# A two-layer transformer kernel: the start of the second attention rearranged (own share by a matrix product, first low part by GpSimd, last normalization one batch later)

## What is computed

```python
xn = _layernorm(x, axis=-1)
s = _L0_attn_ref(xn, ...)              # 16 heads, attention within each token
g = _silu(_L0_ffn_ref(xn, ...))        # 15 experts + last expert's share combine * xn + shared part
x = x + s * g
xn = _layernorm(x, axis=-1)
s = _L1_attn_ref(xn, gamma, w_qkv, w_out)   # rms norm, 16 heads of 64, softmax over 1024 keys
g = _silu(_L1_ffn_ref(xn, ...))
x = x + s * g
```

## Time and profile before

| what | value |
|---|---|
| median of three runs | 1123.43 us (1122.56 to 1123.49) |
| the profiled execution | 1122.48 us, of which its span is 1120.4 us |
| TensorE busy | 1100.0 us, 98% of the span |
| VectorE, GpSimd, ScalarE busy | 847.6, 794.2, 590.7 us |
| granted TensorE clock | 1.000 of full speed |
| stretch of the change | about 311 to 375 us |

### The profile page before, as it was taken

How to read it: one execution, slowest core, us unless ns; L and a number is a source line. 1 busy time by engine, 2 the same in 40 slices (tenths; PEclk the granted TensorE clock), 3 DMA queues, 4 the chain that set the end, 5 groups by cost and what they waited for, 6 DMA issues and landing times.

```text
span 1120.4 us, 21168 instructions
## 1 busy us (share of the span) xinstructions
PE 1100.0 (98%) x8397; PEld 705.2 (63%) x8397; DVE 847.6 (76%) x1250; ACT 590.7 (53%) x936; POOL 794.2 (71%) x522
## 2 busy tenths in 40 slices
PE   9999999999989999999999999999999999999998
PEld 7899989777755555555555455455455455457886
DVE  4777897576585788887887887888888888896554
ACT  4443334567657465465555555555555455554443
POOL 4777878754357889888888888898898898950000
PEclk9999999999999999999999999999999999999999
DMA  7322223210000002000000000000000000000000
GB/s 254 121 78 77 96 78 109 72 51 1 1 1 1 1 1 104 1 1 1 1 1 1 1 1 1 1 1 1 1 1 1 1 1 1 1 1 10 6 5 19
DMA packets 25601, 30.97 MB, mean 28 GB/s; under 512 B 2064, under 2 KB 21904, under 8 KB 24224
## 3 DMA queue, kind: packets, MB, share of 16 engines
q1 hardware_dynamic: 25184, 29.62, 7.9%
q10 hardware_dynamic: 320, 0.01, 0.0%
HBM read 20.19 MB, written 9.44 MB: 26 GB/s over the span
## 4 chain that ended last, share of the span: by engine, by line
PE 86%; DVE 10%; issue 2%; ACT 2%; POOL 1%; DVEq 0%; POOLq 0%; ACTq 0%
PE o_ps L1674 19%; PE mx_ps L1629 7%; PE st_ps L1652 5%; PE st_ps L1658 5%; PE st_ps L1655 5%; PE ha_banks L628 4%; PE bank L2080 3%; PE bank L2081 3%; PE bank L2082 3%; PE mx_ps L1567 3%; PE pj_ps L1586 2%; PE pj_ps L1578 2%; PE ha_banks L687 2%; PE ha_banks L676 2%; DVE mx_part L1892 2%
## 5 line engine op out<-in xcount | busy, mean ns | idle before, releaser
L1994 POOL TENSOR_TENSOR acc<-acc,prob 128x1024 f32<-128x1024 f32 x192 | 468.5, 2440 | 63.6 <-ACT prob L1818 53.4
L1818 ACT ACTIVATE prob<-st_ps 128x1024 f32<-128x1024 f32 x256 | 248.5, 1023 | 208.2 <-PE st_ps L1658 208.2
L1674 PE MATMUL o_ps<-prob,v_cur 128*64 128x512 f32 x1024 | 245.6, 599 | 0.0
L1889 DVE TENSOR_REDUCE mx_part<-mx_ps 128x1 f32<-128x512 f32 x258 | 164.9, 667 | 72.4 <-PE mx_ps L1629 72.4
L1674 PEld LDWEIGHTS o_ps<-prob,v_cur 128*64 128x64 f32 x1024 | 68.0, 136 | 96.3 <-issue 76.4
L1892 DVE TENSOR_REDUCE mx_part<-mx_ps 128x2 f32<-128x1024 f32 x79 | 94.9, 1201 | 44.2 <-PE mx_ps L1629 44.2
L1908 DVE RECIPROCAL rden<-rden 128x128 f32<-128x128 f32 x128 | 120.6, 943 | 0.0
L1629 PEld LDWEIGHTS mx_ps<-k_hi,q_hi 64*128 64x128 f32 x416 | 46.7, 183 | 107.9 <-issue 94.9
L1629 PE MATMUL mx_ps<-k_hi,q_hi 64*128 64x512 f32 x416 | 112.2, 456 | 2.3 <-DVE mx_part L1892 1.9
L1658 PE MATMUL st_ps<-q_hi,d_lo 64*128 64x512 f32 x512 | 100.7, 389 | 0.0
L1994 POOL TENSOR_TENSOR acc<-prob 128x1024 f32<-128x1024 f32 x32 | 76.1, 2378 | 26.7 <-PE pj_ps L1563 18.9
(11 more groups left out here) (415 smaller groups left out, 2355.8 us busy)
## 6 DMA issues: line engine op xcount, KB each, us to landing
v_rows<-ha_v SPq DMA_DIRECT2D x8, 1024.0 KB, 3.9
ha_vt<-v_rows SPq DMA_DIRECT2D x16, 512.0 KB, 4.0
h_w<-in_h SPq DMA_DIRECT2D x2, 1024.0 KB, 7.3
w_raw<-in_w SPq DMA_DIRECT2D x8, 192.0 KB, 3.9
head_wkv<-in_wkv SPq DMA_DIRECT2D x2, 512.0 KB, 4.7
m_w<-in_m SPq DMA_DIRECT2D x3, 256.0 KB, 3.1
out<-fin SPq DMA_DIRECT2D x3, 256.0 KB, 2.3
sel_raw<-in_sel SPq DMA_DIRECT2D x1, 576.0 KB, 10.6
```

The lines of the kernel that those rows point to most:

```text
L1674: mm = pe.matmul(o_ps[rows(h), :], v_cur[:, m % 2, j, rows(h)], prob[:, (16 * m + slot) % RING, h, :], start=(j == 0), stop=(j == KT - 1), ...
L1818: act.activation(prob[:, n % RING, :, :], st_ps[:, slot % 2, :, :], ACT.Exp, scale=SCALE).then_inc(s_exp, 1)
L1889: dve.reduce_max(mx_part[:, h, i, keys:keys + 1], maxima_banks(q, n)[h], AX_X).then_inc(s_mxr, 1)
L1994: pool.tensor_tensor(total, old, new, ALU.add).then_inc(s_acc, 1)
```

## The change

Three things are changed, all in the begin of the second attention and the batches behind it.

1. The last chunk's `own` is added to the bank `y_ps` by TensorE, as a full-precision product with the identity, before the last down products; `gate` is read from the bank. The VectorE step `res` of that chunk is gone. Maximum 3 now stands before these products. `tensor_awake` makes four products and waits for `gate`.
2. The first query projection is copied by ScalarE to `q_raw` (the memory of `res`), which frees its bank for maximum 2; its low part `q_lo` is made by GpSimd from that copy, and the first scores wait for it.
3. `new` and `x` of the last chunk move from the end of the begin to batch (0,1), and `mean`, `cen`, `sq`, `var`, `sd`, `rs`, `spread`, `xn`, `rsq`, `rvar`, `rsd` each one batch later. The mean goes into the bank `n_ps` (that is `pj_ps`) where it used `y_ps`, and takes its place in `pj_uses`. The first outputs wait for `gate` where they waited for `cen`.

```diff
 def tensor_norm(pe, kn, name):
-            pe.matmul(means(kn), c.mean[:, :], x[:, kn, :], start=True, stop=True).then_inc(s_mean, 1)
+            pe.matmul(n_ps, c.mean[:, :], x[:, kn, :], start=True, stop=True).then_inc(s_mean, 1)
 def scalar_norm(act, kn, name):
-            act.wait_ge(s_sum, kn + 1)
-            act.activation(gates(kn)[0], res[:, :], ACT.Silu).then_inc(s_gate, 1)
+            if kn == LAST:
+                act.wait_ge(s_y, ALL)
+            else:
+                act.wait_ge(s_sum, kn + 1)
+            act.activation(gates(kn)[0], y_ps if kn == LAST else res[:, :], ACT.Silu).then_inc(s_gate, 1)
 def tensor_down(pe, n):
+            if t == ALL - 1:
+                pe.wait_ge(s_own, CHUNKS)
+                pe.matmul(y_ps, c.ident[:, :], own[:, :], start=False, stop=False)
 def second_attention(...):
+    q_raw = e.res[:, :]
-    NORMS_AT = {(0, 0): ("mean",), (0, 1): ("cen", "sq"), (0, 2): ("var", "sd"), (0, 3): ("rs", "spread"),
-                (0, 4): ("xn", "rsq", "rvar", "rsd"), (0, 6): ("rclip", "rrs"), (0, 7): ("rspread",),
+    NORMS_AT = {(0, 1): ("gated", "new", "mean"), (0, 2): ("cen", "sq"), (0, 3): ("var", "sd"), (0, 4): ("rs", "spread"),
+                (0, 5): ("xn", "rsq", "rvar", "rsd"), (0, 6): ("rclip", "rrs"), (0, 7): ("rspread",),
                 (1, 0): ("xr",), (1, 1): ("xr_hi",)}
 def unit_out(pe, q, u):
+        elif u[1] == "mean":
+            pe.wait_ge(e.s_cen, CHUNKS)
 def tensor_maxima(pe, q, n):
-                pe.wait_ge(s_lo, 1)
+                pe.wait_ge(s_qraw, 1)
                 pe.wait_ge(s_kall, 1)
 def tensor_scores(pe, m, slot):
             pe.wait_ge(s_d, 1)
+            pe.wait_ge(s_lo, 1)
 def tensor_outputs(pe, m, slot):
-                pe.wait_ge(e.s_cen, CHUNKS)
+                pe.wait_ge(e.s_gate, CHUNKS)
 def tensor_begin(pe):
-        for n in range(1, 3):
+        for n in range(1, 4):
             tensor_maxima(pe, 0, n)
         e.tensor(pe, e.ALL + 1)
-        tensor_maxima(pe, 0, 3)
...
-        tensor_awake(pe, 5)
+        tensor_awake(pe, 4)
 def scalar_begin(act):
         scalar_unit(act, 0, QK[1])
+        act.activation(q_raw, unit_bank(0, QK[1]), ACT.Copy).then_inc(s_qraw, 1)
 def vector_begin(dve):
         vector_maxima(dve, 0, 0)
-        vector_low(dve, 0, QK[1])
...
-        e.vector_norm(dve, LAST, "sum")
...
+        dve.wait_ge(s_lo, 1)
         vector_low(dve, 0, QK[2])
         vector_maxima(dve, 0, 8)
-        e.vector_norm(dve, LAST, "gated")
-        e.vector_norm(dve, LAST, "new")
 def gpsimd_begin(pool):
+        pool.wait_ge(s_qraw, 1)
+        pool.tensor_tensor(q_lo[0][:, 0:CH], q_raw, q_hi[0][:, 0:CH].bitcast(F32), ALU.subtract).then_inc(s_lo, 1)
         gpsimd_cut(pool, 0)
```

More of the change, by code:

```diff
@@ L1055, in gates @@
         return (n_ps, n_ps) if kn < LAST else (gate[:, :], new[:, :])
-    def means(kn):
-        return n_ps if kn < CHUNKS - 1 else y_ps
     def scalar_root_table(act):
@@ L1135, in vector_norm @@
             dve.wait_ge(s_mean, kn + 1)
-            dve.tensor_tensor(centred[:, :], x[:, kn, :], means(kn), ALU.subtract).then_inc(s_cen, 1)
+            dve.tensor_tensor(centred[:, :], x[:, kn, :], n_ps, ALU.subtract).then_inc(s_cen, 1)
         elif name == "rs":
@@ L1312, in gpsimd @@
                                ALU.subtract).then_inc(s_xlo, 1)
-    s.ALL = ALL
+    s.ALL, s.res = ALL, res
     s.tensor, s.scalar, s.vector, s.gpsimd = tensor, scalar, vector, gpsimd
@@ L1322, in experts @@
     s.s_y, s.s_sum, s.s_own, s.s_h, s.s_sg, s.s_su = s_y, s_sum, s_own, s_h, s_sg, s_su
-    s.s_cen, s.s_sd, s.s_xn, s.s_rsd, s.s_xr, s.s_xrlo = s_cen, s_sd, s_xn, s_rsd, s_xr, s_xrlo
+    s.s_gate, s.s_cen, s.s_sd, s.s_xn, s.s_rsd, s.s_xr, s.s_xrlo = s_gate, s_cen, s_sd, s_xn, s_rsd, s_xr, s_xrlo
     return s
@@ L1376, in second_attention @@
     s_qhi, s_lo, s_khi, s_kall, s_d = (at.sem(n) for n in ("s_qhi", "s_lo", "s_khi", "s_kall", "s_d"))
+    s_qraw = at.sem("s_qraw")
     s_dhi, s_dlo = (at.sem(n) for n in ("s_dhi", "s_dlo"))
@@ L1478, in second_attention @@
     pj_uses += [u for m in range(STEPS + 1) for b in range(BATCHES)
-                for u in [maxima_there(m, b), unit_there(m, b), after(m, b)] + norm_at(m, b) if u and u[1] != ("norm", "mean")]
+                for u in [maxima_there(m, b), unit_there(m, b), after(m, b)] + norm_at(m, b) if u]
     turn_of = {turn: n for n, turn in enumerate(pj_uses)}
@@ L1678, in tensor_awake @@
     def tensor_awake(pe, times):
-        pe.wait_ge(e.s_sum, CHUNKS)
+        pe.wait_ge(e.s_gate, CHUNKS)
         for _ in range(times):
@@ L1733, in tensor @@
         for q, u in norm_at(m, b):
-            if u[1] != "mean":
-                bank_free(pe, turn_of[q, u])
+            bank_free(pe, turn_of[q, u])
             e.tensor_norm(pe, LAST, u[1])
```

## The result

| | median us | range | executions |
|---|---|---|---|
| before | 1123.43 | 1122.47 to 1124.23 | 13 |
| changed | 1125.50 | 1124.23 to 1127.04 | 13 |

The ratio is 1.0019, 95% interval 1.0012 to 1.0026: 2.1 us slower. The interval lies wholly above 1, though the difference is just under the 0.2% that the prediction took as the least that can be told from no change. The forecast was 1125.4 (1122.2 to 1126.9).

What follows compares the result with a forecast made beforehand. TensorE, busy 98%, was taken as the bound, with VectorE's chain binding from 312 to 330 us. Terms of +0.3 and +2.1 gave +2.4 on the profiled 1122.48, 1124.9, set at 1125.4 between two scales; range 1122.2 to 1126.9.

Steps and rivals of the forecast that it cites:

- The step that decides: In batch (0,1), `x` starts 0.05 us after GpSimd's add, which holds it; TensorE stalls +2.1 us before the mean product.
- case A: The forecast itself, chance 0.60: `x` in batch (0,1) is held by GpSimd's add; spans +1.5 to +3.2 us.
- Rival B: In batch (0,1), `x` gets in first or the add comes 0.1 us later: +0.3, 1122.8 to 1123.7; chance 0.30.
- Begin: From 312 to 323 us: 0.37 us won at maximum 4 on VectorE, 0.85 in all by maximum 11 on TensorE.
- The mean: Mean product behind the outputs of batch (0,1), no longer in TensorE's gap between maxima 10 and 11: +0.86 us.
- The small terms: In the batches after the begin: waits for `cen` and `xn`, `rvar`'s stall, and `r1clip`'s gap gone; together +0.27 us.
- waits for `cen` and `xn` +0.26: TensorE's next projection waits for `cen`, +0.16 us; a like wait for `xn` in batch (0,5), +0.1.
- `rvar` +0.8 less 0.17: `rvar`, behind the first denominator product, waits for ScalarE's copy `rden`: +0.8 us; its earlier wait for ScalarE goes: -0.17.
- `r1clip` -0.62: In batch (0,6), GpSimd should be idle when `r1clip` comes, so TensorE's 0.62 us idle there goes.
- Sum without meeting or fall: All terms of the begin and the batches after it, without `x` held by the add: +0.3 us.
- Rival C: Own product and mean hide in TensorE's idle of the begin; VectorE's whole 2.6 us come off: 1119.9; chance 0.05.
- D: As case A, plus `r1clip` in batch (0,6) held up to 2.4 us: +3.6, 1126.1 to 1127.0; chance 0.05.

Runs made afterwards that it cites:

- e3: The kernel before with part 3 alone (`new`, `x` and the normalization steps moved one batch later); 1126.62 us, ratio 1.0028.
- changed again: The changed kernel measured and profiled a second time, nothing altered; 1124.05 us, ratio 1.0015.
- e1: The changed kernel with four products without use put between maxima 10 and 11 on TensorE; 1126.6 us, ratio 1.0032.
- e2: Parts 1 and 2 of the change alone, with `new`, `x` and all normalization steps where the kernel before had them; 1122.52 us, ratio 0.9995.
- e11: The changed kernel with `new` and `x` back behind maximum 8 and four products without use between maxima 10 and 11; 1123.38 us, ratio 1.0007.

## Why the prediction was right, and where not

- **The number.** Forecast 1125.4, measured 1125.50, ratio 1.0019. That it was met so closely is partly luck: the first profile stands +1.45 over before by the ruler, the second +3.52, and the forecast's sum of +2.4 lies between them. The 24 times of the changed kernel lie at 1123.7 to 1125.0, 1125.1 to 1126.1 and above 1126.4. The first group has the profile with the fall and `x` free, the last the one with `x` held and a fall near 362 (the other two of its three executions have a mean clock of 0.996, which points to more than one fall). `x` held alone, the forecast's own course, would give +2.2 (3.52 less the 1.3 of that fall) and fit the middle group by its time. But all eight executions of that group have a mean clock of 0.998, where the two of e3 that kept their clock show 1.000. So the middle group is not explained, and no execution of the changed kernel shows the forecast's course by itself.
- **The step that decides** (case A). The mechanism was right and exact where the clock holds: add at +2.40, `x` at +2.46 and 2.87 us long, TensorE's stall 2.04 (forecast +2.41, +2.46, 2.9 to 3.1, 2.1), in three kernels (changed again, e1, e3) with a lead of 0.045 to 0.053 us each. The Trainium skill, SBUF — State Buffer, "SBUF: two separate sides", says that of a VectorE instruction with two SBUF inputs and a GpSimd instruction that reads SBUF the one that starts first has the shared ports for its whole length, and the other waits. The traces agree: `x` took 2.87 us instead of 0.69 beside an add that began 0.05 us before it. Rival B, the add a little late and `x` free, also happened, in the first profile, but by a cause it did not name, whose own price (1.3 us) it did not count.
- **The step that failed** is that the granted clock stays at 1.00. The prediction read 1.00 in the earlier trace rows and carried it over, while it itself moved the mean out of "TensorE's gap between maxima 10 and 11". It priced the mean at its length and did not ask what its leaving does to the gap: 0.27 became 1.32 us of idle, and in some executions the clock fell behind it, for +1.3 us. In the three profiles in which `x` was held in batch (0,1) (changed again, e1, e3), the clock held there and fell behind the `rvar` wait, for +1.3 too. No rival had it. The Trainium skill, TensorE: Matmul & The Clock Gate, "Part 1: The HAM clock gate", says of a kernel's start that the monitor behind the gate runs free of the program, so that how many products run at the low clock changes from run to run. The traces show the like in the middle of a kernel: the same 1.32 us gap was followed by 0.50 in the first profile and by 1.00 in the second.
- **Begin.** Forecast: maximum 4 at 317.2 on VectorE, -0.37; measured 317.30, but with maximum 0 at 311.66, so -0.70 counted from maximum 0 (5.64 us behind it, against 317.62 less 311.28, 6.34). The own product cost what was said: from 313.98 to 315.18 it and one down product take 1.20, and the down product 0.34 (the earlier trace rows and the timeline before, 314.20 to 314.54), so 0.86. What was mis-sized is the maxima ahead of it: maxima 1, 2 and 3 now run side by side in 0.99 us (312.99 to 313.98), where three steps of 0.43 were counted. Maximum 11: -1.25 instead of -0.85, of which e2 shows -0.70 to be parts 1 and 2, and -0.55 the removal of `new` and `x`.
- **The mean** was put at +0.86 from the earlier trace rows; measured +1.06 (335.45 to 336.51, and 334.90 to 335.95 in e11).
- **The small terms** (waits for `cen` and `xn` +0.26, `rvar` +0.8 less 0.17, `r1clip` -0.62; sum +0.27): measured together +0.28, with 0.88 idle before `rvar` and `r1clip` at 0.16.
- **Sum without meeting or fall**: forecast +0.3; e11, which is that case but for `new` and `x` early and a fill, +0.61 at batch (0,7) and 1.0007 in time; with the begin of the changed kernel it would be -1.25 + 1.06 + 0.28 = +0.1. Rival C (all 2.6 us come off) did not occur, nor D.
- **What was missed beside the forecast**: that `r1clip`'s 0.62 us could be won without part 3 at all. It stood in the earlier trace rows of the kernel before.

## What to carry to other kernels

A short product that stands in an engine's gap is not free to move: price its length at the new place, and read what idle it leaves at the old one, with the granted clock behind it. Before a VectorE step with two SBUF inputs is moved, list every GpSimd instruction in reach of the new place, the first of a row as well, since a lead of 0.05 us decides 2 us. When the profiled executions of one program differ by whole mechanisms, read two profiles before explaining a median, and set each execution's mean clock beside its time. Ask also whether parts of a change that lose can be left out: here two parts gained 0.7 us by the ruler, and the third lost over four times that (3.1 us).
